# Expert up products of a gated mixture-of-experts kernel: the first weight matrix read in place by a register address

## The reference

```python
x = x + tanh(g_xattn[0]) * xattn(layernorm(x), ctx, ctx, ...)     # times its own q, then projected
xt = layernorm(x).reshape(-1, 256)
w_topk, sel = top_k(einsum('td,ed->te', xt, gate_w), 2)
combine = zeros((T, 8)).at[arange(T)[:, None], sel].add(softmax(w_topk))
h = silu(einsum('td,edf->tef', xt, w1))          # w1: 8 x 256 x 1024, the "up" products
y = einsum('tef,efd->ted', h, w2)                # w2: 8 x 1024 x 256, the "down" products
x = x + tanh(g_ffn[0]) * einsum('ted,te->td', y, combine)
```

## Time and profile before

| what | value |
|---|---|
| median of 3 runs | 799.15 us (797.16 to 802.18) |
| the profiled execution: its span | 800.5 us, 1.35 us over the median of the runs |
| TensorE matmuls | 754.5 us busy, 8162 instructions |
| TensorE weight loads | 631.8 us busy, 8163 instructions |
| VectorE | 584.1 us busy, 1234 instructions |
| ScalarE | 381.4 us busy |
| GpSimd | 401.6 us busy |
| DMA | 93.70 MB, mean 117 GB/s |

### The profile page before, as it was taken

One profiled execution on the slowest core, in us unless ns is written; L12 is line 12 of the kernel. 1 busy time (PEld: TensorE's weight loads), 2 busy tenths in 40 slices (PEclk: granted clock), 3 DMA queues, 4 the chain that ended last, 5 costly groups with the idle time before them and its releaser, 6 DMA issues. The chain is left out here.

```text
span 800.5 us, 23093 instructions
## 1 busy us (share of the span) xinstructions
PE 754.5 (94%) x8162; PEld 631.8 (79%) x8163; DVE 584.1 (73%) x1234; ACT 381.4 (48%) x680; POOL 401.6 (50%) x380
## 2 busy tenths in 40 slices
PE   4979999999999999996999989899999999999993
PEld 2657777776777677775999878899999999999993
DVE  6669889899998989795767667666666665665660
ACT  3566767767666766652435342333333333333330
POOL 3124454757575667575333738444444444534442
PEclk9999999999999999998999999999999999999998
DMA  8542342536272716233787843233323323233221
GB/s 266 158 132 106 123 150 100 197 111 232 73 265 73 270 49 230 88 152 108 226 232 202 255 106 92 57 53 46 52 46 46 47 45 53 46 46 50 50 28 20
DMA packets 53141, 93.70 MB, mean 117 GB/s; under 512 B 9160, under 2 KB 36880, under 8 KB 53072
## 3 DMA queue, kind: packets, MB, share of 16 engines
q1 hardware_dynamic: 30032, 65.89, 24.7%
q0 software_dynamic: 13392, 18.03, 12.8%
q10 hardware_dynamic: 9648, 8.85, 4.3%
HBM read 53.76 MB, written 37.95 MB: 115 GB/s over the span
## 5 line engine op out<-in xcount | busy, mean ns | idle before, releaser
L1387 PE MATMUL h_ps<-bx_h,w_now 128*128 128x128 f16 x2272 | 196.0, 220 | 0.6 <-DVE w_now L1523 0.6
L1400 PE MATMUL pair_ps<-weights,ht_h 128*128 x1136 | 190.3, 273 | 1.2 <-ACT y L1466 0.6
L1387 PE MATMUL h_ps<-bx_l,w_now 128*128 128x128 f16 x1136 | 157.1, 220 | 0.0
L1387 PEld LDWEIGHTS h_ps<-bx_h,w_now 128*128 128x128 f16 x2272 | 154.4, 98 | 2.5 <-issue 1.3
L1400 PE MATMUL pair_ps<-weights,ht_l 128*128 x568 | 154.8, 273 | 0.0
L1459 ACT ACTIVATE hid<-h_ps 128x1024 f32<-128x1024 f32 x71 | 72.7, 1024 | 156.5 <-PE h_ps L1387 144.4
L1630 POOL TENSOR_TENSOR wait_mark<-wait_mark 128x1 f32<-128x1 f32 x71 | 46.8, 659 | 186.8 <-ACT y L1466 134.8
L1631 POOL DMA_INDIRECT out<-y,meta x71 | 122.8, 1730 | 17.9 <-issue 10.4
L1201 POOL TENSOR_TENSOR r_l<-r,r_h 128x512 f16<-128x512 f32 x64 | 74.5, 1164 | 102.9 <-ACT r_h L813 101.6
L1400 PEld LDWEIGHTS pair_ps<-weights,ht_h 128*128 128x128 f16 x1136 | 110.1, 97 | 15.5 <-issue 1.6
L1529 DVE CAST ht_h<-hid 128x1024 f16<-128x1024 f32 x71 | 49.3, 694 | 100.0 <-ACT hid L1459 99.9
(11 more groups left out here) (261 smaller groups left out, 1336.9 us busy)
## 6 DMA issues: line engine op xcount, KB each, us to landing
stage<-in_w SPq DMA_DIRECT2D x16, 1024.0 KB, 9.1
w_split<-split SPq DMA_DIRECT2D x14, 1024.0 KB, 6.0
weights<-w_split SPq DMA_DIRECT2D x14, 1024.0 KB
rows<-records ACTq DMA_DIRECT2D x67, 129.0 KB
xin<-in_x SPq DMA_DIRECT2D x8, 512.0 KB, 4.9
x_even<-in_x SPq DMA_DIRECT2D x4, 512.0 KB
x_odd<-in_x SPq DMA_DIRECT2D x4, 512.0 KB
out<-x_even SPq DMA_DIRECT2D x4, 512.0 KB
```

The lines of the kernel that those rows point to most:

```text
L1387: last = nc.tensor.matmul(h_ps[r % 2][:, c, :], w1_now[:, r % 2, s, k * F + c * P:k * F + c * P + P], xt[:, r % 2, k, :], start=(j == 0 an ...
L1400: last = nc.tensor.matmul(y_ps[r % 2], ht[:, r % 2, c, :], weights_at(e, s, WN // 2 + c * D, D).rearrange("p o n -> p (o n)"), start=(c == ...
```

## The change

The buffer `w1_now`, the semaphore `w1_ready` and `take_w1` go. `hidden` gets the block's expert as a value in a register of TensorE, waits itself for that expert's loads, and its weight operand is `weights` at the register's address. The order of the six products of a column is changed as well: the half k of D is now the outer loop, and the two products that use the same weights (high part) stand side by side. The sums are the same.

```diff
-    w1_now = sb("w1_now", [P, 2, 2, KD * F], F16)
...
-        def hidden(i, r):
+        def hidden(i, r, e):

             pe.wait_ge(x_lo, i + 1)
             after(pe, h_act, i - 1)
-            pe.wait_ge(w1_ready, i + 1)
+            pe.wait_ge(loads, e * (16 * LOADS) + 1)
             for c in range(FC):
-                for j, (xt, s) in enumerate(((xt_h, 0), (xt_h, 1), (xt_l, 0))):
-                    for k in range(KD):
-                        last = nc.tensor.matmul(h_ps[r % 2][:, c, :], w1_now[:, r % 2, s, k * F + c * P:k * F + c * P + P],
+                for k in range(KD):
+                    for j, (xt, s) in enumerate(((xt_h, 0), (xt_l, 0), (xt_h, 1))):
+                        last = nc.tensor.matmul(h_ps[r % 2][:, c, :], weights_at(e, s, k * F + c * P, P).rearrange("p o n -> p (o n)"),
                                                 xt[:, r % 2, k, :],
                                                 start=(j == 0 and k == 0), stop=(j == 2 and k == KD - 1))
             last.then_inc(h_mm, 1)
...
-            hidden(i, r)
+            hidden(i, r, expert_of(pe, i))
...
-        def take_w1(i, r, e=None):
-
-            e = expert_of(dve, i) if e is None else e
-            dve.wait_ge(loads, e * (16 * LOADS) + 1)
-            after(dve, h_mm, i - 1)
-            nc.vector.tensor_copy(w1_now[:, r % 2], weights[:, bass.ds(e, 1), :, 0:KD * F].rearrange("p o s n -> p (o s) n")).then_inc(w1_ready, 1)
-
...
             if there(i + 1):
-                take_w1(i + 1, (r + 1) % RB)
                 x_low(i + 1, (r + 1) % RB)
             split_h(i, r)

         nc.vector.memset(loads_base[:, :], 0.0).then_inc(loads, 1)
-        first_expert = expert_of(dve, 0)
         x_low(0, 0)
-        take_w1(0, 0, first_expert)
```

More of the change, by code:

```diff
@@ L1304, in experts @@
     loads = sem("weight_loads")
-    xt_mm, x_hi, x_lo, meta_done, w1_ready, h_mm, h_act, h_hi, h_lo, y_mm, y_out, added = (sem(n) for n in (
-        "xt_mm", "x_hi", "x_lo", "meta_done", "w1_ready", "h_mm", "h_act", "h_hi", "h_lo", "y_mm", "y_out", "added"))
+    xt_mm, x_hi, x_lo, meta_done, h_mm, h_act, h_hi, h_lo, y_mm, y_out, added = (sem(n) for n in (
+        "xt_mm", "x_hi", "x_lo", "meta_done", "h_mm", "h_act", "h_hi", "h_lo", "y_mm", "y_out", "added"))
     HEAD = 5 * RB
```

## The result

The changed kernel takes 971.5 us (970.1 to 973.0, 4 runs), the kernel before 798.3 us in the same comparison: a ratio of 1.216, 95% interval 1.212 to 1.221. The forecast was 967 us, in a range of 875 to 1050.

A forecast was written before the change was run, and what follows sets the result against it. TensorE's own stream, 5.52 us a block, was taken as the bound; a sequencer's block of 8.1 us adds 183 us over 71 blocks, less 9 and 6, taking the span from 800.5 to 968.5 and the time to 967 us, range 875 to 1050.

The forecast's parts named there:

- The bound: Expert stage: TensorE's own stream sets the time, 5.52 us a block for 71 blocks; VectorE's copy does not.
- The removal: VectorE's 71 copies and the wait on w1_ready go: 0.6 us gained, between 0 and 14 us.
- the lock of meta: Ahead of x_low: the row copy of meta waits for an older scatter, behind 7.3 us of TensorE's idle.
- The price of an operation: TensorE's queue: each register operation for a weight address takes 0.125 us, read from the down products' rows.
- The bare 46 ns, the lower bound: Hidden products: 32 register operations at 46 ns make 1.5 us, a sequencer's block of 5.6 us, no loss.
- The count of 32: Hidden products: 8 columns x 2 halves of D x 2 parts, 32 register operations for 48 products.
- The sequencer's block: TensorE's queue, one block: transposes' waits, two value loads, hidden, down and loop's end sum to 8.1 us.
- The loop's end: TensorE's queue, once in four blocks: 0.1 us a block allowed, without a row.
- What vanishes: Expert stage: TensorE's waits for other work vanish in a slower beat, 9 us.
- Half of the routing products' 12 us: Expert stage: routing products, 12 us, run half in the new gaps, 6 us off the span.
- From the span to the time: Last step: median 1.35 us under the profiled span, so a span of 968.5 gives 967 us.
- a falling clock: Rival, TensorE in the expert stage: a dry engine granted 1.2 in place of 2.4 GHz, some 1190 us; chance 4%.

The follow-up runs named there:

- the run with 16 columns: The kernel before, but VectorE copies only 16 of the 4096 columns and the up products read expert 0's w1 at a fixed address: 802.5 us, ratio 1.0005.
- the two runs at 805 and 812: The changed kernel with up products at a fixed address, value load and wait kept: 805.5 us; with one register address for all 48: 812.0 us.

## Why the prediction was right

**The bound.** TensorE's stream, and 5.52 us a block: held, since the run without registers has the same beat and the small copy the same time.

**The removal.** 0.6 us, not the 14 of all waits: held by the run with 16 columns (no difference). It was argued from a copy that TensorE had waited for once. The reason given for the waits for bx_l, the lock of meta and not the copy, was half of it: they went when meta was taken later (1.3 us), but also when the copy shrank with the lock in its place (1.2 us). In that trace other waits took their place, and so the number held.

**The price of an operation.** 0.125 us from the down products' rows, carried over to weight loads: 0.129 by the step from 32 to 48, 0.118 from 16 to 32, and 4.2 us for hidden against the 4.0 forecast. The bare 46 ns, the lower bound, was rightly left aside: what counts is the distance of two such operations in a queue that has run dry, and not their duration. The count of 32 was right because the program makes each address once. The Trainium skill (TensorE: Matmul & The Clock Gate, "Wait — 56ns, not 53.3ns?") says that a MATMUL costs about 62 ns where the sequencer's code decodes it and not the hardware. An estimate by this page, had a register address forced that path, is 48 x 62 + 32 x 46 ns = 4.4 us for hidden. The trace speaks against it: in the run with one address 48 products at a register address go in 2.85 us, 59 ns each, as they do at a fixed one.

**The sequencer's block.** 8.1 us forecast, 8.17 measured. The two value loads, 0.9 and 0.8 in the sum, are seen as 0.07 to 0.61 us of gap ahead of hidden and 0.66 to 0.78 ahead of down, as the down products alone (2.8 us executed, 2.0 issued) give the queue a lead that hides part of the first. The loop's end costs more than the 0.1 I allowed: 8.58 less 8.03, the mean of the other three, is 0.55 once in four blocks, 0.14. A value load was worth 0.67 in the run with one, where I had 0.75. So the sum is closer than its terms, which is in part luck.

**What vanishes.** 9 us of waits for other work: held, 1.0 and 3.2 ahead of the stage are all that stay. Half of the routing products' 12 us: the stage lasts from 374.3 to 956.5, 582.2 us, of which 71 x 8.17 are 580.1, so 2 us of them are seen where I said 6. The 5 us more in the blocks and the 4 less here nearly cancel.

**Where it was off.** I expected TensorE's busy share near 80%; it is 90%, for the modelled ends cover most gaps. VectorE stays over 500 us (507.2). And the sum over the block, which is right for a saturated sequencer, is wrong near the balance: it made me expect 790 us for the two runs at 805 and 812. The forecast was not hurt, since 8.1 is far from 5.52.

**From the span to the time.** The profiled span was forecast at 968.5 us and is 969.2. The median time is 2.3 us over that span, and I had taken it 1.35 under, so this step makes most of the 4.5 us between 967 and 971.5. In every run the profiled execution's own time is 1.7 to 1.8 us over its span. The kernel before's span of 800.5 would then belong to its run of 802.2 us, the slowest of the three, and not to one near the median.

## What to carry to other kernels

A register address in an operand is not free on TensorE: each different one cost 0.12 to 0.13 us of its queue once the queue was the bound, more than two products of 128 columns (0.056 each), and each value load 0.67. Before moving a choice of data from an idle engine's copy to the bound engine's addresses, count its register operations and add up the queue over a whole block; the price can be read where such operands already exist. And work that lies beside the bound can be large in the list of groups and give nothing back: the copies, 87.7 us there, were worth no time when they shrank (ratio 1.0005).

## What the hardware showed that was not expected

**A lead that is used up.** In the kernel before, the sequencer was at its limit without showing any wait: one more register operation of 42 ns ahead of the down products went with a kernel 1.2% slower (0.11 us a block). The value load for the down products comes behind the queue's limit (issued at 604.7, first down product 605.54), so what the sequencer does there has only those 0.8 us of cover, whatever room the block as a whole has. That is argued from these rows; no run put the same step elsewhere in the block.

**The clock.** In the changed kernel the granted clock stayed at 1.00 in 600:700. With 48 operations, in blocks of some 10 us, it was at the lower level (1.2 GHz) for stretches; from 600 to 1000 us its mean was 0.85. The table of windows and the chain of that run:

```profile
600.00:1000.00 400.00, 372.32 (x2893) 285.81 (x2892) 94.50 (x156) 69.50 (x117) 67.89 (x78) 0.85 0.16 26
```

In the chain the same 24 products take 4.34 us in one block and 2.81 in the next:

```profile
617.48 4.34 PE pair_ps L1399 x24
...
622.04 5.39 PE h_ps L1386 x48
...
628.21 2.81 PE pair_ps L1399 x24
...
631.30 6.27 PE h_ps L1386 x48
```

It cost little even so (1118 us against 1112 forecast without it). The chain shows why: the hidden products behind the down products of 4.34 us take 5.39 us, those behind the ones of 2.81 us take 6.27, so over half of the 1.5 us that were lost is made up. The queue kept its pace: the 16 register operations of the down products start from 617.4 to 619.4 in the one block and from 628.1 to 630.0 in the next. The prediction had a falling clock as a rival at 4% and argued that gaps under 1 us would keep it up; in this run no gap of TensorE that the waits list was over 0.9 us, and it fell.
